# Expert layer of a two-layer decoder: the router's product with the gate weights held still and 256 rows moving

## The reference, cut to what matters

```python
t = x * rsqrt(mean(x * x, -1) + 1e-6) * norm_weight      # x is already layer-normed here
tokens = t.reshape(-1, 256)                              # 4096 rows
gate_logits = tokens @ gate_w.T                          # gate_w: 8 x 256
gate_scores, expert_idx = top_k(gate_logits, 2)
routing_weights = softmax(gate_scores)
# each row goes through its two experts: w1 (256 -> 512), gelu, w2 (512 -> 256)
out = sum of routing_weights * expert(tokens)
```

## Time and profile before

| | |
|---|---|
| time before, median of 3 runs | 4003.85 us (4002.11 to 4009.77) |
| the profiled execution, its own time | 4002.22 us |
| its span in the trace | 4000.5 us |
| TensorE busy (products) | 3622.6 us, 91% |
| VectorE, ScalarE, GpSimd busy | 2943.7, 2167.8, 300.2 us |
| mean granted clock of TensorE | 0.958 of 2.4 GHz |
| the gate loop, first gate load to the copy of the logits | 1556.38 to 1608.28 us |
| the choice and the scatter | 1608.28 to about 1722 us |

### The profile page before, as it was taken

The page is one execution under the profiler, slowest core; times in us unless marked ns, Lnnn a source line. Parts: engine busy times, 40 slices in busy tenths (PEclk is TensorE's granted clock), DMA queues, the critical chain, the costliest instruction groups (busy, mean ns, idle before and its releaser), DMA issues. The chain is left out here.

```text
span 4000.5 us, 93426 instructions
## 1 busy us (share of the span) xinstructions
PE 3622.6 (91%) x28994; PEld 3018.5 (75%) x28994; DVE 2943.7 (74%) x9189; ACT 2167.8 (54%) x6661; POOL 300.2 (8%) x382
## 2 busy tenths in 40 slices
PE   6999999899999998079877879998799999999998
PEld 5888888688888887069755656666588888888887
DVE  5666666677777775556567768888888888888886
ACT  5777777677777774135344447777333333333333
POOL 0000000000000000521286000000000000000000
PEclk9999999899999997589989889999899999999999
DMA  2000000100000002422211000000200000000000
GB/s 97 0 0 0 0 0 0 47 24 10 10 10 10 16 6 101 132 94 78 71 48 31 0 19 21 16 21 16 93 14 11 13 10 13 8 10 13 10 11 9
DMA packets 56112, 109.74 MB, mean 27 GB/s; under 512 B 8368, under 2 KB 27184, under 8 KB 55728
## 3 DMA queue, kind: packets, MB, share of 16 engines
q1 hardware_dynamic: 46656, 80.72, 6.3%
q0 software_dynamic: 8464, 26.22, 2.0%
q10 hardware_dynamic: 864, 1.19, 0.1%
HBM read 72.46 MB, written 35.65 MB: 27 GB/s over the span
## 5 line engine op out<-in xcount | busy, mean ns | idle before, releaser
L639 ACT ACTIVATE c_pr<-c_sm,c_nmx 128x256 f32<-128x256 f32 x512 | 254.5, 499 | 153.6 <-DVE c_nmx L485 153.6
L127 PE MATMUL f_ps_out<-f_out_rounded,f_zgT 128*128 128x256 f32 x1024 | 310.4, 303 | 0.0
L128 PE MATMUL f_ps_out<-f_out_rest,f_zgT 128*128 128x256 f32 x1024 | 288.7, 282 | 0.0
L129 PE MATMUL f_ps_out<-f_out_rounded,f_zgT 128*128 128x256 f32 x1024 | 286.5, 280 | 0.0
L639 ACT ACTIVATE a_pr<-a_sm,a_nmx 128x128 f32<-128x128 f32 (+1 forms) x512 | 227.3, 445 | 106.0 <-DVE a_nmx L485 105.9
L485 DVE CUSTOM_DVE_ANT_0 a_sm<-a_ps_s,causal 128x128 f32<-128x128 f32 (+1 forms) x512 | 152.6, 355 | 164.2 <-PE a_ps_s L371 164.2
L2151 DVE TENSOR_REDUCE f_v<-f_gv 128x64 f32<-128x512 f32 x256 | 268.6, 1049 | 0.4
L1742 ACT ACTIVATE c_pr<-c_ps_s,c_nmx 128x256 f32<-128x256 f32 x512 | 213.8, 499 | 88.9 <-DVE c_nmx L1574 88.9
L485 DVE CUSTOM_DVE_ANT_0 c_sm<-c_ps_s,c_mask 128x256 f32<-128x256 f32 x512 | 186.8, 421 | 92.0 <-PE c_ps_s L371 90.2
L2301 ACT CAST f_zgT<-f_ps_g 128x512 fp32r<-128x512 f32 x256 | 151.3, 591 | 184.4 <-PE f_ps_g L2031 184.4
L2142 DVE TENSOR_TENSOR f_gv<-f_ps_v,f_gm_step 128x512 f32<-128x512 f32 x256 | 175.2, 684 | 98.1 <-PE f_ps_v L129 86.6
(11 more groups left out here) (377 smaller groups left out, 11442.2 us busy)
## 6 DMA issues: line engine op xcount, KB each, us to landing
f_slot_rows<-f_run POOLq DMA_DIRECT2D x1, 9216.0 KB, 34.9
f_rows<-f_slot_rows SPq DMA_DIRECT2D x72, 128.0 KB, 2.0
f_slot_out<-f_y SPq DMA_DIRECT2D x72, 128.0 KB, 1.9
c_ctx_stage<-in_ctxT SPq DMA_DIRECT2D x32, 256.0 KB, 2.8
small<-in_f_w SPq DMA_DIRECT2D x16, 512.0 KB, 3.9
x_sb<-in_x SPq DMA_DIRECT2D x8, 512.0 KB, 7.9
small<-in_c_w SPq DMA_DIRECT2D x8, 512.0 KB, 3.8
c_mask_stage<-in_mask SPq DMA_DIRECT2D x16, 256.0 KB, 3.0
```

What stands on the lines that cost most here:

```text
L127: nc.tensor.matmul(out, sh, mh, start=start, stop=False, **kw)
L128: nc.tensor.matmul(out, sh, ml, start=False, stop=False, **kw)
L129: return nc.tensor.matmul(out, sl, mh, start=False, stop=stop, **kw)
L639: last = nc.scalar.activation(pr[:, r, i, 0:n], sm[:, j, i, 0:n], ACT.Exp, bias=nmx[:, j, i:i + 1], scale=-1.0, accum_out=sums[:, r, i:i + 1])
```

## The change

The operands of the gate product change places. The gate weights are loaded (8 columns of load) and a whole batch of 256 rows streams past them, so that a batch takes 2 halves x 3 = 6 products, and their result is the logits turned: 8 partitions x 256 columns, in one of the two idle banks `ps_h`. ScalarE copies it to SBUF (`take_lT`, into `lT`, a part of `run[1]` with room for two batches), and TensorE turns it back with two transposes into the places of `ps_l` where the logits lay before (`turn_gates`). TensorE's program becomes, for each `b`, `turn_t(b)`, `gates(b - 1)`, `turn_gates(b - 2)`. ScalarE's becomes its two multiplications for b and then `take_lT(b - 1)`. VectorE waits for the last `l_ps` where it waited for the last `gated`.

```diff
+        lT = run[1][0:E, Q // 2:Q // 2 + 2 * S // E, :].rearrange("p n e -> p (n e)").rearrange("p (k s) -> p k s", k=2)
...
                 if b == 0:
                     pe.wait_ge(pieces.split, 1)
+                if b >= 2:
+
+                    pe.wait_ge(lT_ready, b - 1)
+                for dc in range(DC):
+                    last = product3(nc, ps_h[b % 2][0:E, 0:S], [a[:, dc, :] for a in gate_w],
+                                    [a[:, b % 2, dc, :] for a in tT], dc == 0, dc == DC - 1)
+                last.then_inc(gated, 1)
+
+            def turn_gates(b):
+                pe.wait_ge(lT_ready, b + 1)
                 for i in range(ST):
                     n = ST * b + i
-                    for dc in range(DC):
-                        last = product3(nc, ps_l[:, n * E:(n + 1) * E], [a[:, b % 2, dc, i * P:(i + 1) * P] for a in tT],
-                                        [a[:, dc, :] for a in gate_w], dc == 0, dc == DC - 1)
-                last.then_inc(gated, 1)
-
-            for b in range(B + 1):
+                    last = nc.tensor.transpose(ps_l[:, n * E:(n + 1) * E], lT[:, b % 2, i * P:(i + 1) * P], c.ident[0:E, 0:E])
+                last.then_inc(l_ps, 1)
+
+            for b in range(B + 2):
                 if b < B:
                     turn_t(b)
-                if b:
+                if 1 <= b <= B:
                     gates(b - 1)
+                if b >= 2:
+                    turn_gates(b - 2)
...
-            dve.wait_ge(gated, B)
+            dve.wait_ge(l_ps, B)
...
+            def take_lT(b):
+                act.wait_ge(gated, b + 1)
+                if b >= 2:
+
+                    act.wait_ge(l_ps, b - 1)
+                nc.scalar.copy(lT[:, b % 2, :], ps_h[b % 2][0:E, 0:S]).then_inc(lT_ready, 1)
+
             for b in range(B):
                 act.wait_ge(tT_ps, b + 1)
...
                 last.then_inc(tT_round, 1)
+                if b >= 1:
+                    take_lT(b - 1)
+            take_lT(B - 1)
```

More of the change, by code:

```diff
@@ L751, in routed_experts @@
         gated = sem("gated")
+        lT_ready = sem("lT_ready")
+        l_ps = sem("l_ps")
         made = sem("made")
```

## The result

| | before | after |
|---|---|---|
| time, median of 4 runs | 4006.65 us (4002.11 to 4009.77) | 3981.22 us (3978.32 to 3982.98) |
| ratio, 95% interval | | 0.9938 (0.9926 to 0.9950) |
| span of the profiled execution | 4000.5 us | 3978.9 us |
| gate loop, first gate load to the copy of the logits | 51.90 us | 29.07 us |
| mean granted clock of TensorE | 0.958 | 0.964 |

What follows compares the result with a forecast made beforehand. TensorE at half clock was taken to bound the gate loop. First batch -1.28, thirteen periods -11.9 and tail -0.5 made -13.7 us, from the median 4003.85 to 3990.1 us; range 3983 to 3996.

Steps and rivals of the forecast that it cites:

- The price of a wide product: Gate loop on TensorE: each new product of 256 moving columns costs 0.213 us at half clock, six 1.28 us a batch.
- The copy on ScalarE: Gate loop: the added copy takes 0.35 us a batch on ScalarE but costs nothing, having 0.9 us of slack.
- Rival C: Gate loop: new products run at plain fp32 pace, 0.465 us each, turn 3.92 us; 4013.6 us in all, chance 0.04.
- rival B: Gate loop: new hand-overs between TensorE and ScalarE bind, turn 3.0 us; 3998 us in all, chance 0.09.
- rival A: Gate loop: the clock rises inside the loop, turn 1.96 us; -19 us, 3985 us in all, chance 0.27.
- wide products for only 1.28 of 2.41 us, transposes for most of the rest: Gate loop: argument against the clock rising, as wide products fill only that part of the new turn.
- the floor of the chain: Gate loop: transposes through ScalarE and VectorE to gate products take 2.96 us, so a turn can't be under 2.26 us.
- The tail: End of the gate loop, from the last batch's transposes to VectorE's start on the logits: 6.07 us before, -0.5 us.
- the first batch: Start of the gate loop: `turn_t(2)` stands behind six products instead of twelve, -1.28 us.
- the transposes back: Gate loop on TensorE: two added a batch, 0.178 us each, 0.36 us a batch (0.22 to 0.43).
- the old seam of 0.07: Gate loop on TensorE: 0.07 us left over in each old turn, kept unchanged in the new turn's sum.
- the likeliest case: Gate loop stays TensorE-bound at half clock, turn 2.41 us; 3990 us in all, chance 0.60.

Runs made afterwards that it cites:

- experiment 8: The changed kernel with ScalarE copying each turned result a second time, into an unread place; one run, 3983.68 us.
- experiment 3: The changed kernel with two of its six gate products a batch, those with the rests left out; one run, 3983.79 us.
- experiment 4: The kernel before with eighteen unread wide products a batch added behind its twelve old ones; one run, 4017.68 us.
- experiment 2: The kernel before with 15 unread plain fp32 products ahead of the gate loop, to start it at full clock; 4002.56 us, ratio to before 0.9998.
- experiment 1: The kernel before with the six new wide products a batch added, unread, behind its twelve old ones; 4022.56 us, ratio to before 1.0047.
- experiment 7: The changed kernel with the two feature halves in separate PSUM banks, so VectorE starts after ScalarE's first instruction; 3980.74 us, ratio to before 0.9940.
- experiment 5: The changed kernel with the new way for even batches only, odd batches keeping the twelve old products; one run, 3993.95 us.
- experiment 9: The changed kernel with eighteen unread wide products a batch added; one run, 3994.38 us.

## Why the prediction was wrong

**Right.** TensorE bound the loop before, and each us off the loop came off the span: 22.8 of the loop, 21.6 of the span, the difference being 1.5 us gained ahead of the loop and behind it and 2.7 lost later, 2.5 of them in the linear attention (369.6 us for 367.1). The price of a wide product with 8 columns loaded, 0.213 us at half clock: the starts at 1557.76, 1557.97, 1558.19, 1558.40 of the first turn. The copy on ScalarE is hidden (experiment 8). The choice and the scatter moved as a block. Rival C, the pace of plain fp32, didn't show, nor rival B.

**Wrong, first: the clock (rival A, given 0.27, is what happened).** The step was "wide products for only 1.28 of 2.41 us, transposes for most of the rest", read as too little, from a stretch where wide products with holes between them ran at 0.50 for 9 us. The runs put in its place: the clock rises in this loop, and with all else equal the number of wide products a batch decides. In the old loop it stayed at 0.50 with none and with six, and rose with eighteen; in the new one it stayed at 0.50 with two, and rose with four and with six. The loads of 128 columns don't decide it (experiments 3 and 4), and neither does a start at full clock (experiment 2). A plain share of the turn isn't the rule either, for six in every other batch made it go up and down at a smaller share than the six of experiment 1. How soon it rises in the new loop isn't explained: 4.0 and 4.7 us after the first gate product in the two profiles of the changed kernel, 1.1 us in experiment 7. Nor did any run test why the stretch of the earlier trace rows, from which I had argued, stayed at 0.50 for so long. The rule of the Trainium skill in "TensorE: Matmul & The Clock Gate", Part 1, that sustained matmul activity releases the half clock, came out right here for the new loop, and for the old one, 51 us at 0.50 without a hole, only if its narrow products and their loads aren't counted as such activity. That page's Part 4, by which full clock doesn't engage for transposes, agrees with experiment 3, whose loop is in good part transposes (0.71 + 0.31 of 1.895 us) and stayed at 0.50. No loop here had transposes alone, and those of the changed kernel ran at 1.00 beside its wide products, 0.42 us for four.

**Wrong, second: the floor of the chain.** The step was "`gates(b)` stands at T + 0.70, so T can't be under 2.26", and with it rival A's T = 1.96. It takes a fixed distance between turns for a bound. The runs showed turns of 1.755 us at full clock, below both. `gates(b)` may simply wait; what its lateness delays is `turn_t(b + 2)`, for two batches are in flight. So the turn is half of chain plus gate products plus transposes back, (2.49 + 1.02) / 2 = 1.755 at full clock, as long as that is more than TensorE's own work. Four kernels bear it out (1.755, 1.895, 1.635, 1.565), the last three with the turn told beforehand (1.9, 1.65, 1.55). This made rival A too dear by 0.205 us a turn, 11 x 0.205 = 2.3 us. The tail gave 0.9 us more than rival A had for it (1.93 for 1.0) and the first batch 0.3 (1.55 for 1.28): -19 forecast for it, -22.8 measured.

**Mis-sized terms.** No kernel ran the whole new loop at half clock, so what its steady turn would have been is an estimate. From `turn_t` to the load of the last gate product it is 1.77 us (1576.90 to 1578.67, experiment 5); from there to the transposes back 0.56 (1558.40 to 1558.96 in the changed kernel) and for these 0.31. Together 2.64 us, not 2.41: the transposes fit (0.71 for 0.70) and the transposes back were dear by 0.05, but the products with their seams take 1.63 for 1.35, because the load engine waits ahead of the transposes back, 0.42 us there, for which the sum had nothing but the old seam of 0.07. The one turn that did run at half clock, 2.79, 2.78 and 2.78 us in the changed kernel's two profiles and that of the doubled copy, is longer by 0.15, the early start of its first load, which the first batch had gained (1.55 for 1.28). Had the clock stayed, the loop would by this estimate have been 1.55 + 0.54 + 12 x 0.69 + 0.5 = 11 us shorter: the likeliest case was itself too good by 3 us, and this error and the one of the clock pulled in opposite directions.

How much of the 22.8 us is the clock depends on which is counted first. Places first: about 11 from the change of places at half clock and about 12 from the clock. Clock first: the old loop at full clock was never run for longer than its first turns, but by experiment 9 the change of places is worth 0.20 us a turn there, 3 us, which leaves about 20 for the clock.

**The rest of the range.** 25.4 us between the medians is 2.6 more than the loop gave. Part of it is the start 0.9 us sooner and the 0.55 behind the loop; what is left is within the spread of the linear attention. That spread is larger than the 2 us between the median and the range, and the changed kernel's second median was 3983.67, inside it: on which side of the bound it fell is in part chance. That the likeliest case, 3990, was missed by 9 us is not.

## What to carry to other kernels

Where a stretch is bound by TensorE at half clock although it has no hole, look at what streams. Here narrow products behind wide loads left the clock down, and turning them so that the long side streams won more by the clock than by the instructions saved. Price such a change at both clock levels, and give the higher one its due when the new stream fills a good part of the turn. With two batches in flight the turn is half of one batch's whole round, or the work of the busiest engine if that is longer; a wait of one instruction is no bound by itself. Judge an edit of some us by its own stretch in the trace when another stretch of the same program wanders by 20 us.

## What the hardware showed that I had not expected

The clock fell from 1.00 to 0.50 at 1557.7 in experiment 2, in the middle of uninterrupted products and loads. The eighteen products with which it rose in experiment 4 had only eight output partitions each. Narrow products behind a weight load of 128 columns in fp32r follow the clock: they start 0.111 us apart at full (experiment 2) and 0.213 at half clock. A transpose of 8 partitions by 128 columns costs 0.11 us at full (1566.15 to 1566.37 for two) and 0.155 at half clock (1558.96 to 1559.27).
